# A four-layer graph network in sixteen hand-ordered groups: every engine's order of steps, and the PSUM bank of each product tile, written anew

## What is computed

```python
# --- layer 0: out = einsum('bik,bkl->bil', softmax(masked e, axis=1), h) + x @ self_weight
# --- layer 1: masked softmax attention, layernorm, adjacency sum, two-layer MLP with layernorm
# --- layer 2: masked softmax attention over leaky_relu(f1 + f2), + bias, elu
# --- layer 3: out = (A * I) @ (x @ W[0]) + (A * (1 - I)) @ (x @ W[1]) + bias
for layer in (L0, L1, L2, L3):
    h = jnp.maximum(_layernorm(x, axis=-1), 0.0)
    x = x + layer(h, adj, ...)
```

## Time and profile before

| | |
|---|---|
| median of 3 runs | 1016.21 us (1014.95 to 1017.24) |
| profiled execution, span | 1013.8 us |
| busy TensorE / VectorE / ScalarE / GpSimd | 94% / 85% / 62% / 55% |
| granted TensorE clock, mean | 0.98 |
| data written by stores | 8.39 MB |

### The profile page before, as it was taken

The page is one execution under the profiler, slowest core; times in us unless marked ns, Lnnn a source line. Parts: engine busy times, 40 slices in busy tenths (PEclk is TensorE's granted clock), DMA queues, the critical chain, the costliest instruction groups (busy, mean ns, idle before and its releaser), DMA issues. The chain is left out here.

```text
span 1013.8 us, 21212 instructions
## 1 busy us (share of the span) xinstructions
PE 949.6 (94%) x7355; PEld 902.1 (89%) x7355; DVE 859.2 (85%) x2526; ACT 632.5 (62%) x1655; POOL 555.4 (55%) x1171
## 2 busy tenths in 40 slices
PE   5989999999999999999999999998999999997998
PEld 4779998988998889899989899998999898886897
DVE  5988897989979988977888888799988989779874
ACT  3347547686668653775686664877548584677741
POOL 3535264582575652765566565654636744467850
PEclk9978999999999999999999999999999999999999
DMA  5020000000020010011000101101000100000003
GB/s 135 1 63 1 1 2 1 2 1 1 2 83 2 1 43 2 1 37 49 2 1 2 43 1 43 43 2 33 11 1 2 42 2 2 21 1 2 1 1 105
DMA packets 38071, 19.99 MB, mean 20 GB/s; under 512 B 3142, under 2 KB 37452, under 8 KB 37964
## 3 DMA queue, kind: packets, MB, share of 16 engines
q1 hardware_dynamic: 36080, 18.42, 6.5%
q10 hardware_dynamic: 1884, 0.21, 0.2%
HBM read 10.23 MB, written 8.39 MB: 18 GB/s over the span
## 5 line engine op out<-in xcount | busy, mean ns | idle before, releaser
L686 PE MATMUL ps<-HE,PT 128*128 128x129 f32 x2048 | 238.5, 276 | 3.2 <-issue 1.9
L686 PEld LDWEIGHTS ps<-HE,PT 128*128 128x128 f32 x2048 | 233.1, 192 | 5.4 <-issue 4.8
L451 ACT ACTIVATE Y<-X,SM 128x128 f32<-128x128 f32 x512 | 204.0, 491 | 49.3 <-POOL SM L447 49.1
L1307 DVE SCALAR_TENSOR_TENSOR PT<-ps,CE,maskT 128x512 f32<-128x512 f32 x256 | 174.2, 742 | 19.2 <-PE ps L810 11.8
L432 POOL TENSOR_TENSOR SM<-ST 128x8 f32<-128x8 f32 x96 | 29.5, 307 | 269.4 <-DVE ST L1170 269.3
L443 POOL TENSOR_TENSOR SM<-SM,minus_half 128x8 f32<-128x8 f32 x96 | 163.3, 1701 | 7.6
L686 PE MATMUL ps<-W,HT 128*128 128x128 f32 (+1 forms) x768 | 126.1, 311 | 0.0
L686 PEld LDWEIGHTS ps<-W,HT 128*128 128x128 f32 x768 | 115.6, 193 | 8.9
L1170 DVE BATCH_NORM_STATS2 ST<-X 128x6 f32<-128x128 f32 x512 | 104.8, 278 | 3.1 <-DMA X<-in_x_dram 0.4
L703 PE MATMUL ps<-ident,Y 128*128 128x128 f32 x640 | 85.6, 278 | 10.7 <-ACT Y L451 10.2
L703 PEld LDWEIGHTS ps<-ident,Y 128*128 128x128 f32 x640 | 72.2, 143 | 16.3 <-ACT Y L451 14.4
(11 more groups left out here) (260 smaller groups left out, 2335.6 us busy)
## 6 DMA issues: line engine op xcount, KB each, us to landing
X<-in_x_dram SPq DMA_DIRECT2D x32, 256.0 KB, 3.5
out_dram<-X SPq DMA_DIRECT2D x32, 256.0 KB, 2.8
adj_raw<-in_adj_dram SPq DMA_DIRECT2D x4, 256.0 KB, 3.5
W<-in_L_gnn_W_dram SPq DMA_DIRECT2D x2, 64.0 KB, 3.8
W<-in_L_gnn_W_dram SPq DMA_DIRECT2D x1, 128.0 KB, 3.6
bias<-in_L_gnn_bias_dram SPq DMA_DIRECT2D x2, 64.0 KB, 4.1
Wo<-L_gnn_others_weight_dram ACTq DMA_DIRECT2D x1, 64.0 KB, 3.1
feat1w<-in_L_gnn_Wp_dram ACTq DMA_DIRECT2D x1, 64.0 KB, 3.5
```

Of the source, the lines that this page charges most:

```text
L451: a = nc.scalar.activation(dst[:, n, 0:F], src[:, n, 0:F], func, scale=SM[s][:, S_RSTD, n:n + 1], bias=SM[s][:, S_SHIFT, n:n + 1])
L686: return nc.tensor.matmul(o, w, m, start=start, stop=stop, skip_group_check=True)
L1307: a = V.scalar_tensor_tensor(out=PT[r][:, j, :], in0=o, scalar=CE[s][:, c:c + 1], in1=maskT[:, j, :].bitcast(F32), op0=ALU.max, op1=ALU.mult)
```

## The change

It puts other strings into `TURNS` for all five queues and another string into `HOMES`. The counts of characters are the same, so each engine takes the same steps with the same instructions on the same operands; only the order across groups and the banks differ. No function is touched. Of the diff, the string of SP whole and the first line of two others:

```diff
 TURNS = {
-    "pe": ("gggg0110101020g2120012413240303410101033114040511522553305120232123223032304143130550100001110404151"
+    "pe": ("gg0gg0121210100g210014124320301031041301301011522353554402025123122330230214140303003005510141104125"
...
-    "sp": ("403510617228394a5b6c7d8e9fadcbef"),
+    "sp": ("453006112728394a5b6c7d8e9ffdcabe"),
...
-HOMES = ("0123456701234567012347056123412341235641702356415670415067125304304356717204356072071241207431256074"
+HOMES = ("0123456701234567012345601234750675067340125673450612734612734506450612732745016071450763276145032761"
```

More of the change, by code:

```diff
@@ L136 @@
-    "pool": ("01201043120153240135234010521430510021421562374626234736847783865384547989a596a96755a679ab67687b87bc"
-           "ab98da89c8adbcae9cdde9ebc9ebdabfcfafefdcdfcebfdefcdbecfdefef"),
-    "sp": ("403510617228394a5b6c7d8e9fadcbef"),
-}
-HOMES = ("0123456701234567012347056123412341235641702356415670415067125304304356717204356072071241207431256074"
[L141 to L148, removed]
@@ new lines @@
+    "pe": ("gg0gg0121210100g210014124320301031041301301011522353554402025123122330230214140303003005510141104125"
+           "4514515421040242015152152236236246242237667434772627623333433443364645487876448665878667878377377858"
+           "58348848849595559659956a5a9a956a6a79979699669565696757aa8767776778b7aba7abbaa96b86aa86bb87788798a8b8"
+           "cabc8bc8b9cd9dabbdcab9dd8989989a9ca9aacaa9eaecacdcdcecbeebdccdedeb9dd9bdde9ebebeceeebbfcfbbdffafdaff"
+           "bcbcafffdffdfccfcceccedcdddcdffddeebffdceeeefefeffefbffbfedcdcfdefefe"),
@@ new lines @@
+    "act": ("0g02112g01g01442303011002131050541130012021540313220133021120503200021413411105524455020124204311212"
+           "43556324623254476327434622572343334347664438586687537866547733687785488447685998595556a9a768a6695796"
+           "76995895666579a77789b7778ab9a68aa67b966b8aa78787ac8a9b8a8bca9dcbb98daab9d8b9c889a99aaaaedecbcb9ccebd"
+           "bedccb9dd9ab9eceddcbbeedcefefbdbbacfdadfaeccefbdffdfccbffcccededffdddcffeeffcbecefeefdefffbdfdcefdef"
+           "efe"),
+    "dve": ("0g21gggg10201g0g004131210001114522300314100131230132220530533414102552423312300214140350420550015123"
+           "0410405511421411022504316531254724362562422226673637427476662333338434576447378746386465888767888774"
+           "46387583588946479559a8599956a7a89995566aa595999676568a9577aaab667976787766baab97aabb7b76886abbc78ba7"
+           "a898d8bac8cb8b89d98bdcacadd989bc899acea9ccad9aabacbecdddecce9bee9cddeeeddbb9acd9eecefebadbedfbcfbfff"
+           "adfffebbccbafffbfdedccfccecdfdfcdcfdceeffddeeefdfdfbfeeffffeceeddbfefce"),
@@ new lines @@
+    "pool": ("0210104310213250431235401021540513002121465273642276346384778358638475499a896a596557a976ba786b6b78a7"
+           "cb98dca98d8acb9ecaddebe99cebdfabafefcdfcbdfcbedfcefedfdcfeef"),
+    "sp": ("453006112728394a5b6c7d8e9ffdcabe"),
+}
+HOMES = ("0123456701234567012345601234750675067340125673450612734612734506450612732745016071450763276145032761"
+         "0456327632764532321032107645132176453210764510324576241031501376241762417650324032417650363653024171"
+         "6530271430214753053201457326405132641370524614626142637015426301754261723015746236250125012743650143"
+         "2743276501403140134027652762756256276251342057346153720461513476250134762476247652013201347652013401"
+         "7652017634520524176305274152360135260127643527643502150125764301301304257613045721304572130421567306"
+         "7342015346207134565620713427134025671567340125673401253467012510251025346701234675467456012735642735"
+         "6423576423051764051235125317642051736424230561742307461523746101524367015462735460127354643564013274"
+         "0561356274027135640546271327123712712305462713654130654271306542716530427163506354271067315421542067"
+         "3154067321523406175324061324032406175403621632175460463217632176504326532046532046560456107456107")
```

## The result

The changed kernel takes 1021.0 us in the median of 18 runs (1016.5 to 1033.5), the kernel before 1015.0 in the same set (1012.4 to 1019.9): a ratio of 1.0057, 95% interval 1.0044 to 1.007, or 5.8 us slower. Two later sets with the same kernel read 1.0054 (1.0023 to 1.0086) and 1.0027 (1.0011 to 1.0043). The mean of the other 34 is 1019.7 us, that of the kernel before 1015.1. So the change costs 3 to 6 us; the forecast was 4.3.

A forecast was written before the change was run, and what follows sets the result against it. TensorE, 94% busy, was taken as the bound. Terms 3.3 + 1.5 + 0 - 0.5 + 0 = +4.3 us on the runs' median of 1016.2 gave 1020.5 us, range 1010.5 to 1028 us.

The forecast's parts named there:

- the gap of 8 us: Sign: 8 us instead of 4.7 between the last matmul and the end of the span.
- the row of DMAs behind the wait for f: Sign: SP waits for group f's store, then issues ten DMAs in a row.
- The end of the stores: After the last matmul: f's store, now first in SP's strict queue, holds back d, c, a, b; +3.3 us.
- Layer 2 to 3 of e and f: Near the end: TensorE waits on VectorE's chain ahead of c.agg3 and d.agg3; +1.5 us, low 0, high +4.
- 1.9 us for `f.elu2b`: First piece of VectorE's 8.6 us chain, counted from the end of f.att2b on TensorE.
- 900 to 950 us: Between e.mlpc1 and e.norm2: 2.7 us less work against 2.7 us less chain; zero, bounds -3 to +3.
- The beginning: Up to 0.agg0: 0.norm0 fills a 0.96 us TensorE wait; -0.5 us, bounds -2 to +1.
- The body: 108 to 900 us: no side seen, TensorE idle stays near 29.9 us; 0 ± 6 us.
- The clock: TensorE's low-clock stretches, three of 27.2 us at 0.50 in all, taken as unchanged.
- the count of tight hand-overs: Hand-overs between TensorE steps with little work between: 65 of 384 before, 60 now; missing work 71 and 77 us.
- The end costs nothing: Rival: both end terms vanish through slack and the stores ride along; about 1016 us, no change; chance 0.13.
- The body packs better: Rival: a quarter of the 36.7 us idle from 43.6 to 900 us goes; 1011.5 us; chance 0.27.

The follow-up runs named there:

- e2: The kernel before with only SP's last six stores reordered to e, d, c, a, b, f; ratio to the kernel before 1.0039, 4.0 us.
- e6: The kernel before for TensorE's first 374 steps, then the new order and banks, with stores in VectorE's finishing order; ratio to the kernel before 1.004.
- e4: The kernel before up to the start of f.norm1, then the new order, banks and store order; ratio to the kernel before 1.018, 18 us.
- e1: The changed kernel with only SP's last six stores reordered to VectorE's finishing order (a, d, b, f, c, e); ratio to the kernel before 0.9996.
- e5: The new order and banks up to the end of 9.feat3, then the kernel before with its old store order; ratio to the kernel before 1.0001.
- e7: The same kernel as e1, run again in a later set; ratio to the kernel before 1.0017.
- e11: e1 plus two VectorE swaps, f.cmax0 ahead of c.mlps1 and 7.top2 ahead of 9.gat1; ratios to the kernel before 0.9951 and 0.9964.
- e10: e1 plus f.cmax0 ahead of c.mlps1, 0.split0 and 0.low0 ahead of eturn (VectorE), 0.agg0 earlier (TensorE), banks changed; ratio to the kernel before 1.0057.

## Why the prediction was right, and where not

The direction, and the stores as the main cost, were right. That 1020.5 us lies 0.5 from the measured 1021.0 is luck: the kernel before is 1015.0 over 18 runs, not the 1016.2 of three, and the difference 5.8, not 4.3. Over all runs the difference is 4.6 us, but of the two positive terms only the stores were there; the +1.5 of the second stood for about 1 us that no run locates. Of the signs named in advance, the gap of 8 us, the full DMA share, the row of DMAs behind the wait for f and the 9.7 ± 3 us idle came; TensorE idle ahead of `c.agg3` or `d.feat3` did not.

**The end of the stores** (+3.3 forecast) measured 3.8 us in the profile, 4.0 in `e2`, 3.6 over all runs. The rate of 286 GB/s was right. Seen in slices of 0.5 us, the data ran from about 1002.6 to 1013.8: 3.15 MB in 11.2 us. The 0.5 us missing is for the most part the start: f was complete at T - 4.5, not T - 5.0, and the data began at about T - 3.6, not T - 4.0; the rest is the length, 11.2 us for 11.0. By the 358 GB/s of the Trainium skill (page "DMA: Bandwidth & Descriptors", section "Where 436 GB/s comes from") the term would have been +1.1, an estimate; the trace shows 286 GB/s and 3.8 us, and decides.

**Layer 2 to 3 of e and f** (+1.5 forecast) measured nothing: 0.2 us idle from 950 us on. The step that failed is "1.9 us for `f.elu2b`", counted from the end of `f.att2b`. Lines of VectorE and, last, of TensorE:

```profile
962.20 0.16 DVE L1352 TENSOR_SCALAR SM<-ps 128x2 f32<-128x2 f32 x1 [0.20 <-issue]
...
965.42 1.23 DVE L1367 SCALAR_TENSOR_TENSOR HE<-HE,X 128x1024 f32<-128x1024 f32 x1 [1.17 <-ACT HE L1029]
973.78 0.41 DVE L1460 TENSOR_TENSOR LOW<-ps,HI 128x256 fp32r<-128x256 f32 x1
974.25 0.44 PE L686 MATMUL ps<-HI,a_hi 128*128 128x256 f32 x1
```

`f.att2b` ends at 963.2, and `f.elu2b` is under way from 962.20: it reads each half when it is written, and the exponential is back at 965.42, 2.2 us behind `f.att2b` where I had 3.5. The last LOW of `c.feat3` is over at 974.19, and `c.agg3` starts at 974.25, just as TensorE's own work ends. I had read the two steps as one after the other. That is 1.3 us of the chain, all of the 1.1 that I had as lost first. Only 0.06 us lie between the two, so the term stood on the edge: its low end of 0 was the right one.

**900 to 950 us** (0): 8.3 us idle and 1.7 of low clock, 10.0 together where there were 9.7. Right.

**The beginning** (-0.5): over the first 56 steps -2.1 us as timed and +1.4 without the low clock, each just outside the bounds of -2 and +1. Wrong was that nothing but the filled wait would differ up to `0.agg0`. It starts 1.2 us earlier (69.52 against 70.76), but TensorE now waits 4.3 us for `0.low0` ahead of it, where it waited 2.7 us for `2.cmax0` and 0.4 for `0.low0`.

**The body** (0 ± 6): 30.8 against 29.9 us idle. Right, and the count of tight hand-overs, which showed no side, was a fair witness.

**The clock** "unchanged" was wrong in each stretch of the two profiles and about right in their sum. At the end of the first 374 steps five profiles of the new order had lost 10.2 to 17.1 us by it, two of the old 18.8 and 20.5; but `e6`, in the old order up to there, had lost 15.4, so the two overlap. Behind this place the new order lost 3.4 to 5.2 us and the old 0 and 5.1. From 50 to 60 us the kernel before lost 5.1 us and the changed one 3.4, although by the prediction's count the run of steps with few columns ahead of it is 1.8 us longer. (In `e2`, `e4` and `e6` the old order lost 3.4 there too, in `e1`, `e5` and `e7` the new one 1.7.) By the Trainium skill's page "TensorE: Matmul & The Clock Gate", Part 4, as weighed in the prediction, it would have lost 0.9 us more, an estimate; no run here bears that out.

**Rivals.** "The end costs nothing" was right for the chain of e and f, and fell with `e1` and `e2` for the stores. "The body packs better" did not happen by itself, but `e11` shows that 5 us lay in it: two swaps. What stays open: the forecast sum was 4.3 us, and stores and order give 3.6 + 1.0 over all runs, each known to about 2 us; the first set's 5.8 is 1 us above that, and whether this is the order, or its typical clock (mean 0.9777 in 34 runs against 0.9788), can't be told from the profiles: the first two of the changed kernel (1016.6 and 1017.3 us) fell on its faster executions.

## What to carry to other kernels

Put stores in the order in which their inputs are complete: in a strict queue one early name holds back all behind it, and what piles up is paid at the end at the DMA rate (286 GB/s here), with nothing to cover it. When an order written out by hand is changed, list TensorE's longest single waits (here 2.4 to 4.3 us) and look one step ahead on the engine that is waited for: two swaps of neighbours gained 5 us where the whole new order gained none. Before a step is moved back, ask which queue waits for its *end*: in `e10` it was the loads of three groups.

## What was not expected of the hardware

**VectorE and GpSimd hold each other up.** Small instructions of VectorE of 0.17 us last 1.89 and some 2.4 us, to the very end of a GpSimd instruction on 128 x 1024 elements that began at the same moment (562.84 + 1.90 = 564.74 against 562.87 + 1.89 = 564.76). In `e11` it goes the other way: GpSimd's L447, 0.20 us elsewhere, lasts 1.14 us beside VectorE's L1322 of 1.23. The Trainium skill, page "SBUF — State Buffer", section "SBUF: two separate sides", says that the two share a pair of ports by an exclusive lock, and that the loser waits for the whole instruction; by that rule, the trace agrees. Moving the small ones ahead of the large one made them fast again, which shows the cause to be their company and not their operands.

**The time at the lower clock differs between executions of one kernel.** Nine profiles hold the same new order on every engine up to 109 us; by then they had lost 6.8, 8.5, five times 10.2, 13.7 and 15.4 us (the last is also what the profile of the kernel before had lost), and the runs' times follow the clock: the changed kernel with its stores in turn took 1011.0 us at a mean of 0.984 and 1020.9 at 0.976 (`e1`). One profile doesn't tell whether a change has moved the clock, and the intervals of twelve runs here are ±2 us.
